# The 16-head attention stage of a two-layer decoder: ScalarE copies the projected keys out of PSUM instead of VectorE

## The chip, the cores and the metric

The kernel runs on one core of a Trainium2 chip. The metric is the device time of one execution in microseconds, lower is better. A core has TensorE (PE, matrix products), VectorE (DVE), ScalarE (ACT) and GpSimd (POOL), each with its own instruction queue in program order; SyncE (SP) here only issues DMA transfers. The engines wait for each other through semaphores. TensorE writes its results to PSUM, eight banks of 128 partitions by 512 float32 values, and VectorE and ScalarE read them there.

## The reference

Everything is float32. Tokens: batch 4, sequence 512, width 256. The decoder has two layers; after each block comes `x = layernorm(x + block(x))`.

```python
x = LN(x + L0_attn(x))            # one head of 256, rotary table
x = LN(x + L0_xattn(x, ctx))      # one head of 256, causal and padding mask
x = LN(x + L0_ffn(x))             # mixture of 8 experts, top 2
x = LN(x + L1_attn(x))            # 16 heads of 16, causal
x = LN(x + L1_xattn(x, ctx))      # 16 heads of 16, mask per query and key
x = LN(x + L1_ffn(x))             # 6 small layers: local attention and gated MLP
```

The two blocks of 16 heads, which the change touches, compute (the second with the context for keys and values and with biases on all projections):

```python
q, k, v = split(x @ Wq.T), split(x @ Wk.T), split(x @ Wv.T)   # (B, 16, 512, 16)
scores = einsum('bhqd,bhkd->bhqk', q, k) / sqrt(16)
scores = where(causal, -1e9, scores)      # cross: where(mask == 0, -1e9, scores)
out = einsum('bhqk,bhkd->bhqd', softmax(scores), v)
return merge(out) @ Wo.T                  # cross: + bo
```

## The kernel before, in words

The kernel is a row of stages. `stage_wide` does the two attentions of 256, `stage_moe` the experts, `stage_heads` both attentions of 16 heads, and `stage_l1_ffn` the six small layers, which take most of the time. The change lies in `stage_heads` alone, from about 486 to 1212 us.

`stage_heads` goes through eight batches of 512 tokens: four of the self attention (`j` 0 to 3), then four of the cross attention (`j` 4 to 7, `cross(j)` is true). A batch is 16 groups, `n` = 0 to 15: four query tiles `t` of 128 tokens, and in each four groups of four heads. In a self batch a tile `t` needs only `(t + 1) * 128` keys, in a cross batch all 512.

`body()` writes the order of the steps out by hand, once for a batch, and every engine walks through the same list, doing its own part of each step. The second entry of a step is the batch that it works for, relative to the one at hand: the projections of the next batch (offset 1) lie between the groups of this one. A prologue (`it` = -1) does them for the first batch, and the last batch has none to do. The steps of a group are, in this order:

- `s`: PE computes the scores of the four heads (L1988) into banks 4 to 7. It first waits until all four are drained.
- `max` 0 to 3: VectorE adds the mask and takes the row maximum (L2172), which drains a score bank; behind the fourth it scales the maxima for ScalarE (`h_nb`, L2177).
- `e` 0 to 3: ScalarE takes the exponentials of the group before (L2087), with a read of the row sum.
- `pt` 0 to 3: PE transposes the probabilities of the second-last group (L1998) into banks 2 and 3 in turn; ScalarE copies numbers 0 and 2 to `h_pT`, VectorE 1 and 3 (L2055).
- `pv`: PE multiplies probabilities and values of the third-last group (L2022).
- In between (`first` in the code, behind `max` 1, `e` 1 and `pt` 1): `q` and `k`, a projection on PE (L1964) into bank 0, then its copy to `h_qT` by ScalarE (L2074 with a bias, L2077 without) or to `h_kT` by VectorE (L2124 with, L2127 without); every fourth group (3, 7, 11, 15) `den` and `div`, where ScalarE copies the raw output (`h_o_raw`, L2102) and VectorE divides it (`h_oT`, L2201); one group later `wo`, the output projection.

The key steps `k` stand in groups 2, 6, 10 and 14, those of the queries in 1 and 9:

```python
            units = {1: ("q", 0), 2: ("k", 0), 6: ("k", 1), 9: ("q", 1), 10: ("k", 2), 14: ("k", 3)}
...
            yield from [("max", 0, n, 0), ("max", 0, n, 1), ("pt", of(m), m, 0), ("e", of(e), e, 0),
                        ("e", of(e), e, 1), ("pt", of(m), m, 1), *first, ("max", 0, n, 2), ("max", 0, n, 3),
                        ("pt", of(m), m, 2), ("e", of(e), e, 2), ("e", of(e), e, 3), ("pt", of(m), m, 3), *second]
```

In the self batches the input of the attention is itself still being made, from the sums of the experts' outputs: GpSimd fetches rows by an indirect DMA into `s_got`, VectorE adds them up (L1364) and normalises (L1382). These steps (`mix`) stand in groups 6 and 12 of the first two batches, and in the prologue.

Of the kernel before, what the change touches and what calls it, by code (L numbers as in the profile page):

```python
# [7 lines left out]
ALU = mybir.AluOpType  # L8
ACT = mybir.ActivationFunctionType
# [1728 lines left out]
def stage_heads(nc, shared, w_self, w_cross, preload, expert_sum):  # L1738
# [15 lines left out]
    with ExitStack() as ctx:  # L1754
# [9 lines left out]
        kT = sb("kT", [P, 2, QC, S])  # L1764
        v = sb("v", [P, 2, 2, TB, D])
# [74 lines left out]
        for step in full:  # L1840
            kind = step[0]
# [16 lines left out]
        def cross(j):  # L1858
            return j >= NB
# [6 lines left out]
        phases, ps = [], None  # L1866
        for it in range(-1, BODIES + 1):
            ps = Psum(shared, it, ps, True)
# [19 lines left out]
        def wait_filled(eng, ps, key, it):  # L1888
            eng.wait_ge(ps.sem_filled(key), ps.count(key, it))
# [168 lines left out]
        def _(act):  # L2058
            act.wait_ge(w_self["landed"], w_self["loads"])
            for steps, ps, it in phases:  # L2060
                if it == NB - 1:
                    act.wait_ge(w_cross["landed"], w_cross["loads"])
                for step in steps:
                    kind, off = step[:2]
                    j = it + off
# [4 lines left out]
                    elif kind == "q":  # L2070
                        e = step[2]
                        wait_filled(act, ps, step, it)
                        if cross(j):
                            ins = nc.scalar.activation(qT[:, j % 2, e, :], ps.ap(step), ACT.Identity,  # L2074
                                                       bias=w_cross["bq"][:, e:e + 1])
                        else:
                            ins = nc.scalar.copy(qT[:, j % 2, e, :], ps.ap(step))  # L2077
                        ins.then_inc(ps.sem_drained(step), 1)
                    elif kind == "e":
                        m, i = step[2:]  # L2080
                        n = group(it, m)
# [23 lines left out]
        def _(dve):  # L2105
# [3 lines left out]
            for b in range(2):  # L2109
                for parity in range(2):  # L2110
                    ins = nc.vector.memset(of_parity(v[:, b, parity], 1 - parity), 0.0)
            ins.then_inc(pads, 1)
            dve.wait_ge(w_self["landed"], w_self["loads"])
            for steps, ps, it in phases:
                if it == NB - 1:
                    dve.wait_ge(w_cross["landed"], w_cross["loads"])
                for step in steps:
                    kind, off = step[:2]
                    j = it + off
                    if kind == "k":  # L2120
                        e = step[2]
                        wait_filled(dve, ps, step, it)
                        if cross(j):
                            ins = nc.vector.tensor_scalar(kT[:, j % 2, e, :], ps.ap(step), w_cross["bk"][:, e:e + 1],  # L2124
                                                          None, ALU.add)
                        else:
                            ins = nc.vector.tensor_copy(kT[:, j % 2, e, :], ps.ap(step))  # L2127
                        ins.then_inc(ps.sem_drained(step), 1)
                    elif kind == "v":
                        i = step[2]  # L2130
                        wait_filled(dve, ps, step, it)
                        src = ps.ap(step).rearrange("p (t d) -> p t d", t=2)
                        for parity in range(2):
                            out = of_parity(v[:, j % 2, parity, 2 * i:2 * i + 2, :], parity)
                            if cross(j):
                                bias = w_cross["bv"][:].unsqueeze(1).broadcast_to([P, 2, D])
# [365 lines left out]
```

## Time and profile before

| | before |
|---|---|
| device time, median of 3 runs | 4149.62 us |
| the 3 runs | 4148.56 to 4154.87 us |
| the profiled execution, its own time | 4142.27 us |
| its span, first to last instruction | 4140.4 us |
| mean granted TensorE clock | 0.979 of full |
| busy PE / DVE / ACT / POOL | 3869.0 / 2905.0 / 2580.3 / 1239.8 us |

A row of the timeline gives the start in us from the span's beginning, the busy time, the engine, the line, the operation with the tile that it writes and those that it reads, shape and count (PE rows of one kind are merged, and a float32 matmul makes two of them). In brackets stands how long the engine was idle before it, and which instruction ended that. Busy shares are means over stages with different limits, so a stage is read from its own stretch.

### The profile page before, as it was taken

Reading aid. Unit: us, or ns where it says so; the run is one execution under the profiler, and the core shown is the slowest. Engines: PE = TensorE matmul, PEld = TensorE weight load, DVE = VectorE, ACT = ScalarE, POOL = GpSimd, SP = SyncE. Lnnn points to the kernel's source line nnn. Section 1 sums busy time; section 2 is a strip of 40 time slices with the busy share of each in tenths; the row PEclk is TensorE's granted clock in tenths of the full one; section 3 lists DMA queues with packets and bytes.
Section 4 is the critical chain, followed back from the end, with each engine's and each line's share of the span. In section 5 each row is a group of like instructions: output and inputs, shape, how many; then the busy total and the mean of one; then the engine's idle time right before and its main releaser. Section 6 shows DMA issues by size and latency. Waiting matters only on the chain.

```text
span 4140.4 us, 97849 instructions
## 1 busy us (share of the span) xinstructions
PE 3869.0 (93%) x36632; PEld 2539.5 (61%) x36632; DVE 2905.0 (70%) x10279; ACT 2580.3 (62%) x6856; POOL 1239.8 (30%) x809
## 2 busy tenths in 40 slices
PE   8979787899988999999999999999999999999996
PEld 5658554566655566666666666666666666666664
DVE  3542377788868878777777777777777777777773
ACT  2213265677756767667677676776766767767662
POOL 1103200000015443434343434343434343434330
PEclk9979899999999999999999999999999999999998
DMA  6002300000011001110011101110011101111010
GB/s 182 24 21 76 111 7 8 14 17 19 7 53 25 17 22 53 28 41 19 17 52 27 43 17 54 30 34 23 23 47 32 38 22 43 28 40 29 17 37 18
DMA packets 110784, 146.32 MB, mean 35 GB/s; under 512 B 35748, under 2 KB 77200, under 8 KB 109936
## 3 DMA queue, kind: packets, MB, share of 16 engines
q1 hardware_dynamic: 106912, 130.76, 11.1%
q0 software_dynamic: 3408, 9.31, 0.9%
q8 instruction: 299, 4.90, 0.5%
q14 instruction: 165, 1.35, 0.1%
HBM read 78.31 MB, written 11.40 MB: 22 GB/s over the span
## 4 chain that ended last, share of the span: by engine, by line
PE 54%; DVE 10%; POOL 4%; issue 2%; DMA 1%; ACT 0%; SPq 0%; DVEq 0%; POOLq 0%
PE psum L489 17%; PE psum L586 10%; PE psum L469 7%; PE psum L570 6%; PE psum L603 5%; PE psum L549 4%; PE psum L523 4%; POOL f_rn L892 3%; DVE f_rot L710 2%; DVE f_prob L753 1%; DVE f_rot L712 1%; DVE f_ss L717 1%; DVE f_xn L807 1%; PE psum L592 1%; DVE f_prob L781 1%
## 5 line engine op out<-in xcount | busy, mean ns | idle before, releaser
L489 PE MATMUL psum<-f_wqkv,f_xsT 128*128 128x512 f32 x2304 | 1073.0, 595 | 4.3 <-ACT f_raw L636 2.7
L887 POOL TENSOR_TENSOR f_raw<-f_rot 128x512 f32<-128x512 f32 x384 | 488.8, 1273 | 1662.4 <-DVE f_rot L712 1662.4
L650 ACT ACTIVATE f_prob<-f_prob,f_nb,f_rq 128x128 f32<-128x128 f32 x1536 | 740.0, 487 | 36.3 <-DVE f_nb L766 35.4
L489 PEld LDWEIGHTS psum<-f_wqkv,f_xsT 128*128 128x128 f32 x2304 | 402.5, 191 | 333.9 <-issue 329.0
L892 POOL TENSOR_TENSOR f_rn<-f_ss,f_half_pow 128x32 f32<-128x32 f32 x96 | 524.4, 5462 | 11.2
L586 PE MATMUL psum<-f_xnT,f_w 128*128 128x512 f32 x960 | 436.9, 594 | 2.2 <-ACT f_hT L673 1.1
L753 DVE CUSTOM_DVE_ANT_0 f_prob<-psum,f_band 128x128 f32<-128x128 f32 x1536 | 352.7, 285 | 114.9 <-PE psum L523 113.8
L634 ACT ACTIVATE f_sq<-psum 128x512 f32<-128x512 f32 x384 | 227.8, 593 | 230.2 <-PE psum L489 230.2
L781 DVE TENSOR_SCALAR f_prob<-f_prob,f_rs 128x128 f32<-128x128 f32 x1536 | 341.4, 286 | 13.5
L570 PE MATMUL psum<-f_wo,f_oT 128*128 128x256 f32 x1536 | 347.4, 379 | 1.6 <-ACT f_v L636 0.9
L710 DVE TENSOR_TENSOR f_rot<-f_raw,f_tab 128x512 f32<-128x512 f32 x384 | 333.0, 867 | 14.8 <-DMA x_before_mlp<-x_all 14.8
L570 PEld LDWEIGHTS psum<-f_wo,f_oT 128*128 128x128 f32 x1536 | 289.8, 190 | 71.3 <-issue 35.7
L2087 ACT ACTIVATE h_prob<-h_prob,h_nb 128x512 f32<-128x512 f32 (+3 forms) x512 | 324.7, 639 | 0.0
L586 PEld LDWEIGHTS psum<-f_xnT,f_w 128*128 128x128 f32 x960 | 178.9, 191 | 209.3 <-issue 200.3
L650 ACT ACTIVATION_READ_ACCUMULATOR f_prob<-f_prob,f_nb,f_rq 128x1 f32 x1536 | 294.7, 192 | 0.0
L1998 PE MATMUL psum<-ident,h_prob 128*128 128x128 f32 x1664 | 247.5, 280 | 50.2 <-DVE h_pT L2055 36.3
L1998 PEld LDWEIGHTS psum<-ident,h_prob 128*128 128x128 f32 x1664 | 182.0, 141 | 176.9 <-issue 94.1
L661 ACT COPY f_oT<-psum 128x512 f32<-128x512 f32 x192 | 111.5, 581 | 285.3 <-PE psum L549 285.2
L683 DVE COPY f_pT<-psum 128x512 f32<-128x512 f32 x192 | 131.9, 687 | 190.1 <-PE psum L469 189.8
L2055 ACT COPY h_pT<-psum 128x512 f32<-128x512 f32 (+3 forms) x256 | 129.0, 504 | 216.3 <-PE psum L1998 215.7
L712 DVE TENSOR_TENSOR f_rot<-f_raw,f_tab 128x512 f32<-128x512 f32 x384 | 262.4, 683 | 0.0
L717 DVE TENSOR_REDUCE f_ss<-f_sq 128x8 f32<-128x512 f32 x384 | 259.9, 677 | 0.0
(247 smaller groups left out, 7080.7 us busy)
## 6 DMA issues: line engine op xcount, KB each, us to landing
f_v_near<-f_v SPq DMA_DIRECT2D x168, 256.0 KB, 3.4
f_wqkv<-in_Wqkv SPq DMA_DIRECT2D x36, 512.0 KB, 6.7
w_moe_W<-in_L_ffn_W SPq DMA_DIRECT2D x2, 4096.0 KB, 23.5
f_w<-in_W SPq DMA_DIRECT2D x12, 640.0 KB
f_wo<-in_Wo SPq DMA_DIRECT2D x6, 1024.0 KB, 6.4
f_xs<-x_all SPq DMA_DIRECT2D x24, 254.0 KB
expert_rows<-m_y SPq DMA_DIRECT2D x39, 128.0 KB, 1.7
h_mask_int<-in_mask_BxSxS_ik SPq DMA_DIRECT2D x16, 256.0 KB
```

Source lines behind the costliest of these rows:

```text
L489: mm = nc.tensor.matmul(ps.ap(step), xsT[:, c, t * P:(t + 1) * P], wqkv[:, c, i * HALF:(i + 1) * HALF], start=c == 0, stop=c == KC - 1)
L570: mm = nc.tensor.matmul(ps.ap(step)[:, 0:D], oT[:, c, :], wo[:, c, :], start=c == 0, stop=c == OC - 1)
L586: mm = nc.tensor.matmul(ps.ap(step), w1[:, c, at:at + P], xnT[:, c, :], start=c == 0, stop=c == KC - 1)
L650: ex = nc.scalar.activation(pr, pr, ACT.Exp, bias=nb[:, t % 2, h:h + 1], scale=rq8[:, t, h:h + 1], accum_out=sums[:, t % 2, h:h + 1])
L710: nc.vector.tensor_tensor(heads(rot[:, n % 2, 0, :]), heads(q), cos, ALU.mult)
L712: nc.vector.tensor_tensor(rot[:, n % 2, 1, :].rearrange("p (h two d) -> p h two d", two=2, d=DH // 2), swapped, sin.rearrange("p h (two d) ...
L753: red = nc.vector.tensor_tensor_reduce(prob[:, (4 * n + 2 * j + i) % 16, :], ps.ap(key)[:, (n % 2 * 2 + j) * P:(n % 2 * 2 + j + 1) * P], b ...
L781: ins = nc.vector.tensor_scalar(pr, pr, rs[:, t % 2, h:h + 1], None, ALU.mult)
L887: nc.gpsimd.tensor_tensor(raw[:, (4 * t + i) % 8, :], rot[:, n % 2, 0, :], rot[:, n % 2, 1, :], ALU.add).then_inc(rope_done, 1)
L892: nc.gpsimd.tensor_tensor(rn[:, t % 2, :], ss[:, t % 2, :], half_pow[:], ALU.pow).then_inc(rn_ready, 1)
L1998: mm = nc.tensor.transpose(ps.ap(step)[:, k * P:(k + 1) * P], prob[:, n % 3 * HPC + i, k * P:(k + 1) * P], ident[:])
L2087: nc.scalar.activation(pr, pr, ACT.Exp, bias=nb[:, t % 2, h:h + 1], scale=scale, accum_out=sums[:, t % 2, h:h + 1]).then_inc(exp_ready, 1)
```

## The change

For the step `k` the branch moves from VectorE's program to ScalarE's. Without a bias ScalarE makes a copy, with one an activation of the kind Identity with the bias column. What is waited for and what is signalled is the same. TensorE's, GpSimd's and SyncE's programs are unchanged.

```diff
@@ scalar @@
                             ins = nc.scalar.copy(qT[:, j % 2, e, :], ps.ap(step))
                         ins.then_inc(ps.sem_drained(step), 1)
+                    elif kind == "k":
+                        e = step[2]
+                        wait_filled(act, ps, step, it)
+                        if cross(j):
+                            ins = nc.scalar.activation(kT[:, j % 2, e, :], ps.ap(step), ACT.Identity,
+                                                       bias=w_cross["bk"][:, e:e + 1])
+                        else:
+                            ins = nc.scalar.copy(kT[:, j % 2, e, :], ps.ap(step))
+                        ins.then_inc(ps.sem_drained(step), 1)
                     elif kind == "e":
@@ vector @@
-                    if kind == "k":
-                        e = step[2]
-                        wait_filled(dve, ps, step, it)
-                        if cross(j):
-                            ins = nc.vector.tensor_scalar(kT[:, j % 2, e, :], ps.ap(step), w_cross["bk"][:, e:e + 1],
-                                                          None, ALU.add)
-                        else:
-                            ins = nc.vector.tensor_copy(kT[:, j % 2, e, :], ps.ap(step))
-                        ins.then_inc(ps.sem_drained(step), 1)
-                    elif kind == "v":
+                    if kind == "v":
                         i = step[2]
```

VectorE's order at the key step of group 2 of the second cross batch, as a piece of the difference. The rows L2055 and L2172 around it are the copy of transposed probabilities 1 and the masked maximum 2 with its read-out.

```order
 L2172 ISA h_mx 128x1
 L2055 COPY h_pT<-psum 128x512
-L2124 TENSOR_SCALAR h_kT<-psum,w_x_bk 128x512
 L2172 ISA h_prob,h_mx<-psum,h_add_mask 128x512
 L2172 ISA h_mx 128x1
```

The key copy is gone from between them; the rest of VectorE's order is the same.

ScalarE's order at the same place after the change, where the exponentials stand on L2096 and the key copy with its bias on L2083.

```order
L2055 COPY h_pT<-psum 128x512
L2096 ACTIVATE h_prob,h_sums<-h_prob,h_nb 128x512 x2
L2083 ACTIVATE h_kT<-psum,w_x_bk 128x512
L2055 COPY h_pT<-psum 128x512
L2096 ACTIVATE h_prob,h_sums<-h_prob,h_nb 128x512 x2
```

The row L2083 is new; without it the two exponentials were followed at once by the copy of transposed probabilities 2.

ScalarE's order in the prologue, before (first piece) and after (second piece).

```order
L2069 COPY h_xT<-psum 128x512 x2
L2077 COPY h_qT<-psum 128x512 x2
L2069 COPY h_xT<-psum 128x512 x2
```

```order
L2069 COPY h_xT<-psum 128x512 x2
L2077 COPY h_qT<-psum 128x512
L2086 COPY h_kT<-psum 128x512 x2
L2077 COPY h_qT<-psum 128x512
L2086 COPY h_kT<-psum 128x512 x2
L2069 COPY h_xT<-psum 128x512 x2
```

Four key copies have come in here, two behind each query copy.

## Rows read from the trace of the kernel before

**Rows 1.** Groups by form, VectorE, then ScalarE (busy, mean ns | idle before, releaser).
```profile
L2124 DVE TENSOR_SCALAR h_kT<-psum,w_x_bk 128x512 f32<-128x512 f32 x16 | 12.0, 748 | 9.6 <-PE psum L1964 9.6
...
L2127 DVE COPY h_kT<-psum 128x512 f32<-128x512 f32 x16 | 11.0, 689 | 17.2 <-PE psum L1964 17.2
...
L2074 ACT ACTIVATE h_qT<-psum,w_x_bq 128x512 f32<-128x512 f32 x8 | 5.5, 688 | 2.1 <-PE psum L1964 2.1
L2077 ACT COPY h_qT<-psum 128x512 f32<-128x512 f32 x8 | 4.7, 587 | 17.5 <-PE psum L1964 13.7 <-remote 3.8
```
**Rows 2.** One stretch: length, busy us PE, PEld, DVE, ACT, POOL, PE clock, DMA.
```profile
937.00:1031.00 94.00, 86.86 (x988) 58.44 (x978) 76.35 (x218) 66.33 (x169) 3.49 (x2) 1.00 0.06 18
```
**Rows 3.** Who waited for whom, 500 to 770 us, then 770 to 1190.
```profile
PE psum L1988 <- DVE h_mx L2172: 12.7, 22, 1.1
...
PE psum L1988 <- DVE h_mx L2172: 16.4, 34, 0.7
```
**Rows 4.** Timeline, second cross batch: end of group 1, group 2, start of group 3.
```profile
936.21 1.07 PE L2022 MATMUL psum<-h_pT,h_v 128*32 128x128 f32 x31
...
937.21 1.14 PE L1988 MATMUL psum<-h_kT,h_qT 32*128 32x512 f32 x8
...
939.21 1.88 PE L1964 MATMUL psum<-h_srcT,w_x_Wk 128*128 128x512 f32 x4
...
941.13 0.75 DVE L2124 TENSOR_SCALAR h_kT<-psum,w_x_bk 128x512 f32<-128x512 f32 x1 [0.74 <-PE psum L1964]
941.57 0.59 ACT L2055 COPY h_pT<-psum 128x512 f32<-128x512 f32 x1 [0.59 <-PE psum L1998]
...
941.90 1.08 PE L2022 MATMUL psum<-h_pT,h_v 128*32 128x128 f32 x32
...
943.13 0.17 DVE L2177 TENSOR_SCALAR h_nb<-h_mx 128x4 f32<-128x4 f32 x1
...
943.25 1.14 PE L1988 MATMUL psum<-h_kT,h_qT 32*128 32x512 f32 x8 [0.27 <-DVE h_mx L2172]
...
945.01 0.59 ACT L2055 COPY h_pT<-psum 128x512 f32<-128x512 f32 x1 [1.44 <-PE psum L1998]
```
**Rows 5.** Timeline, starts of groups 2 and 3 of the last batch.
```profile
1122.72 1.14 PE L1988 MATMUL psum<-h_kT,h_qT 32*128 32x512 f32 x8
...
1127.61 1.14 PE L1988 MATMUL psum<-h_kT,h_qT 32*128 32x512 f32 x8
```
**Rows 6.** Timeline, what follows groups 6, 10, 14 (third self batch), 6 (cross).
```profile
709.85 0.71 PE L1988 MATMUL psum<-h_kT,h_qT 32*128 32x256 f32 x8 [0.52 <-DVE h_mx L2172]
...
710.97 0.37 ACT L2055 COPY h_pT<-psum 128x256 f32<-128x256 f32 x1 [1.16 <-PE psum L1998]
...
727.32 0.93 PE L1988 MATMUL psum<-h_kT,h_qT 32*128 32x384 f32 x8 [0.60 <-DVE h_mx L2172]
...
748.87 1.14 PE L1988 MATMUL psum<-h_kT,h_qT 32*128 32x512 f32 x8 [0.43 <-DVE h_mx L2172]
...
967.07 1.14 PE L1988 MATMUL psum<-h_kT,h_qT 32*128 32x512 f32 x8 [0.24 <-DVE h_mx L2172]
```
**Rows 7.** Timeline, after group 6 of the first, second and fourth self batch.
```profile
536.00 0.71 PE L1988 MATMUL psum<-h_kT,h_qT 32*128 32x256 f32 x8 [0.77 <-DVE h_mx L2172]
...
619.50 0.48 DVE L1364 SCALAR_TENSOR_TENSOR x_all<-s_got,s_gates,x_all 128x256 f32<-128x256 f32 x1 [1.25 <-DMA s_got<-expert_rows,s_slot_int]
...
785.34 0.71 PE L1988 MATMUL psum<-h_kT,h_qT 32*128 32x256 f32 x8 [0.58 <-DVE h_mx L2172]
```
**Rows 8.** Timeline, prologue's end and first groups.
```profile
508.27 1.40 DVE L1382 TENSOR_SCALAR x_all<-x_all,s_mv,s_rstd 128x256 f32<-128x256 f32 x4 [1.16 <-POOL s_rstd L1354]
...
509.59 0.67 DVE L2127 COPY h_kT<-psum 128x512 f32<-128x512 f32 x1
...
510.47 0.81 PE L1988 MATMUL psum<-h_kT,h_qT 32*128 32x128 f32 x8 [4.37 <-DVE h_kT L2127]
...
518.35 0.59 ACT L2077 COPY h_qT<-psum 128x512 f32<-128x512 f32 x1 [3.78 <-remote]
```
## The prediction

> **What bounds the kernel now.** I read the page first, then the stage of the change through the busy times of a stretch, the list of waits, and the timeline of single groups. Over the stretch of [rows 2], which lies in the 512-key part, TensorE (PE) is busy for 86.86 of 94 us, VectorE (DVE) for 76.35 and ScalarE (ACT) for 66.33. No engine is full. PE is nearest to it, and ACT has the most room: 28 us in 94. What PE loses, it loses where a group hands over to the next: the score matmuls (L1988) wait for VectorE's last row maximum of the group before, because all four score banks must be drained. In the list of waits this is 12.7 us in 22 waits up to 770 us and 16.4 us in 34 waits after it [rows 3], 29.1 us together. That sum is the most that a lighter VectorE can give back there, and a part of it belongs to groups in which no keys are copied.
>
> The timeline of one group with a key copy shows the order of events [rows 4]. The scores start at 937.21. PE projects the keys from 939.21 to 941.09 and VectorE, idle for 0.74 us until then, copies them from 941.13. Only behind that copy come its maxima 2 and 3. The scaled maximum (L2177) starts at 943.13, and the next scores start at 943.25, after PE has waited 0.27 us. PE's last work of the group, the probabilities times the values (L2022), started at 941.90 and took 1.08, so it was over at 942.98. So VectorE is the later one here, and it is late by the key copy: it stood idle until the projection was there, though the scores for its maxima had long been filled.
>
> **What the change removes.** VectorE loses 16 plain copies of 689 ns and 16 with a bias of 748 ns, 23.0 us of busy time [rows 1]. Its maxima 2 and 3 no longer queue behind the projection. In the group of [rows 4] they may start 1.4 us earlier (the idle 0.74 and some 0.66 until the next start), more than PE's wait. PE's own work then sets the start of the next scores, and the gain is the wait that stands on that row. It was there because of VectorE alone: the last batch has no key projection, and there group 2 lasts from 1122.72 to 1127.61, 4.89 us [rows 5], against 6.04 us in [rows 4] (937.21 to 943.25). The difference, 1.15 us, is less than the projection's 1.88 us, since part of the projection fills gaps of PE.
>
> There are 32 key copies: 4 in the prologue and 4 in each of the seven batches that prepare a next one. By place:
> - Cross batches 1 to 3 (512 keys): 0.27 us at groups 2, 10 and 14 [rows 4], which repeat, and 0.24 us at group 6 [rows 6]. 1.05 us a batch, 3.2 us in all.
> - Third self batch: 0.52, 0.60 and 0.43 us at groups 6, 10 and 14 [rows 6]. At group 2 PE did not wait, so I count nothing. 1.6 us. The fourth is the same with 0.58 at group 6 [rows 7], 1.6 us.
> - Second self batch: 0.60 and 0.43 as before, 1.0 us. Group 6 gives nothing, because VectorE stands in group 7 for expert rows that GpSimd fetches: 1.25 us before the first of eight additions [rows 7], and the others wait too. An earlier VectorE only waits longer.
> - First self batch: 0.77 us at group 6 [rows 7], 0.60 and 0.43 behind it, and for group 2, which stands beside a stall (below), 0.6 by its neighbour, group 10. 2.4 us.
> - Prologue: the first scores (510.47) waited 4.37 us for the fourth key copy [rows 8], which VectorE could do only behind a normalisation that began at 508.27 and took 1.40. ScalarE is free there, so the scores move ahead of the end of the normalisation. Then VectorE's maxima can start at 509.67 and the transposes queued on PE behind the scores can too, against 510.47 plus the scores' own 0.81 before, that is up to 1.6 us. I take 1.5.
>
> The sum is 3.2 + 1.6 + 1.6 + 1.0 + 2.4 + 1.5 = 11.3 us. Where PE does not wait its rows overlap by 0.07 us (the row at 936.21 ends at 937.28, the scores start at 937.21 [rows 4]), and 24 hand-overs may gain that on top, 1.7 us at most. Between 11.3 and 13.0 I take 12.5 us.
>
> **What it adds.** ScalarE gets 32 instructions. Its nearest rows are the query copies, the same forms from the same PSUM banks: 587 ns plain and 688 ns with a bias [rows 1], so 16 × 0.587 + 16 × 0.688 = 20.4 us of busy time. In its order the key copy stands ahead of the copy of transposed probabilities 2, with exponentials 2 and 3 and, in the next group, the copy of transposed probabilities 0 behind it. In the group of [rows 4] that probability copy started at 941.57 after 0.59 us of idle time, since PE issues its transposes behind the key projection. The keys are full at 941.09, so the new copy begins in this hole at about 941.13 and pushes the probability copy to at most 941.82, by 0.25 us. The exponentials behind it end as much later. Nobody meets them before group 3, in which ScalarE stood idle for 1.44 us until PE's transposes came (945.01, [rows 4]). With PE's start 0.27 earlier and ScalarE 0.25 later, 0.9 us are left. The tightest of the other places is group 7 of the self batches: 1.16 us of idle time [rows 6], less 0.52 for the earlier start and at most 0.3 for the later end. The cost on the path is nothing as long as these holes stand. If the cover were gone, each copy would cost its 0.59 to 0.69 us. The next group after each key group is a divide group (3, 7, 11, 15) and its length hangs on ScalarE's chain, which starts with PE's scores. So that group keeps its length, and what the key group gained stays gained.
>
> No wait is added to PE or to a DMA queue. The bank of the keys is drained by whichever engine copies them, at about the same moment.
>
> **The rivals.**
> *It gains less, within 0.2%.* The first groups stand beside stalls that no engine of this kernel releases: ScalarE waited 3.78 us at 518.35 "remote" [rows 8]. If that stall ends at a fixed moment, the prologue's 1.5 us and the first group 2's 0.6 are lost, and if the 0.07 do not add, 11.3 − 2.1 = 9.2 us are left. One more half-clock stretch of PE, or half of the gains in the self batches (6.6 us by the list) missing, brings it to some 6 us: 4143.6 us.
> *It gains more.* Were VectorE the bound in key groups and just behind them, each copy would give back all its time: 23.0 us less the 2.8 of the prologue, 20 us, 4129.6 us. For it speaks that the waits of [rows 3] sum to 29.1 us. Against it, PE in [rows 4] is late by itself 0.27 us earlier.
> *It gets slower.* ScalarE's copies land on the chain of the divide groups: copy 0, two exponentials, the raw output copy, then VectorE's division and maxima. This decides once ScalarE comes later than PE's transposes, that is when its delay exceeds the idle time left in [rows 4] and [rows 6]. Then 28 copies cost 16 × 0.688 + 12 × 0.587 = 18.1 us and nothing is gained: 4167.7 us. The 0.59 us hole and the 1.16 and 1.44 us behind it speak against this.
> The Trainium skill says in "ScalarE: Activation LUTs", Rules for kernel authors, that an addition is work for VectorE and not for ScalarE; by that rule the change would lengthen the work that it moves. In [rows 1] the same forms take 688 ns against 748 and 587 against 689, so here the measurement decides against the rule.
> The Trainium skill's "Runtime: NRT & Kernel Launch", Instruction fetch mechanics, has each engine fetch its instructions in blocks of 256, mostly hidden; 32 more on ScalarE and 32 fewer on VectorE would move the places of such fetches, and no row shown ties the "remote" stall to them.
>
> **How the numbers follow.** The gain of about 12.5 us: 0.62. More, some 20 us: 0.08. Less, some 6 us: 0.22. Slower: 0.08. The profiled execution took 4142.27 us, and the sum makes that 4129.8. It lies 7.35 us under the median of the runs shown, 4149.62, from which I subtract the same 12.5: 4137. The range reaches from the rival with more (4129.6, less a little for the half-clock stretches, whose places move with the time) to a gain close to nothing: 4128 to 4149. The slower rival is left out. 0.2% of this time, 8.3 us, is about what a measurement of this kernel can tell from no change. Faster by more than that: 0.70, within it 0.22, slower 0.08.
>
> **What the profile would show.** VectorE has 32 instructions and 23 us less in the stage. The wait of the scores for VectorE after groups 2, 10 and 14 of a cross batch is gone and such a group lasts 5.7 instead of 6.04 us, while the divide groups keep theirs. The key copy on ScalarE starts within 0.1 us of the projection's end, and ScalarE's idle time before copy 0 of the next group is shorter but not gone. The prediction is wrong if that idle time is zero, if a new wait of PE for ScalarE's probability copy appears, or if the stall near 518 us grows.

## The result, and the profile after

| | before | changed |
|---|---|---|
| median of 20 runs each, taken together | 4152.34 us | 4143.08 us |
| lowest and highest | 4141.97 to 4158.32 | 4139.10 to 4152.14 |
| profiled execution, its own time / its span | 4142.27 / 4140.4 us | 4144.43 / 4142.4 us |
| mean granted TensorE clock of that execution | 0.979 | 0.974 |

The ratio is 0.9983, with the interval 0.9976 to 0.9989: the change is faster, by 0.17%, some 7 us (the means, 4151.7 and 4144.1, lie 7.6 us apart, the medians 9.3). Two later comparisons, which stand with the experiments, gave 0.9979 [0.9970, 0.9988] and 0.9977 [0.9968, 0.9986], that is 9 to 10 us. The profiled execution of before is as fast as the fastest of its 20 runs (4141.97) and had a higher clock, 0.979, than any of the 105 later runs of that kernel (0.973 to 0.978). So its span cannot be compared with the one of after. What can be compared are groups of the stage in which both ran at full clock.

The page of the changed kernel gives the load of each engine:

```profile
span 4142.4 us, 97849 instructions
...
PE 3881.6 (94%) x36632; PEld 2548.2 (62%) x36632; DVE 2886.2 (70%) x10247; ACT 2602.4 (63%) x6888; POOL 1240.4 (30%) x809
```

VectorE lost 19 us of 2905, ScalarE gained 22 of 2580. The groups by form show the new instructions (busy, mean ns | idle before, releaser), against [rows 1]:

```profile
L2083 ACT ACTIVATE h_kT<-psum,w_x_bk 128x512 f32<-128x512 f32 x16 | 11.0, 689 | 3.7 <-PE psum L1964 2.5
...
L2086 ACT COPY h_kT<-psum 128x512 f32<-128x512 f32 x16 | 9.4, 588 | 15.5 <-PE psum L1964 15.3
```

Here they take 689 and 588 ns, 20.4 us in all, where 688 and 587 were expected from the query copies. The stretch of [rows 2], read again:

```profile
937.00:1031.00 94.00, 87.89 (x1001) 58.77 (x989) 74.13 (x215) 69.76 (x176) 3.48 (x2) 1.00 0.06 18
```

In 94 us PE works 1.03 us more, VectorE 2.2 less, ScalarE 3.4 more. The list of waits, up to 770 us and then from 770 to 1190, answers to [rows 3]:

```profile
PE psum L1988 <- DVE h_mx L2172: 6.8, 12, 0.7
...
PE psum L1988 <- ACT h_kT L2086: 0.9, 1, 0.9
...
PE psum L1988 <- DVE h_mx L2172: 12.6, 19, 0.7
```

The waits of the scores for VectorE's maxima fell from 29.1 us in 56 waits to 19.4 us in 31. None of the 31 that are left stands at the start of group 3, 7, 11 or 15, that is behind a key group. The timeline of the second cross batch shows the same group as [rows 4]:

```profile
937.31 1.14 PE L1988 MATMUL psum<-h_kT,h_qT 32*128 32x512 f32 x8
...
939.31 1.88 PE L1964 MATMUL psum<-h_srcT,w_x_Wk 128*128 128x512 f32 x4
...
941.01 0.68 DVE L2172 CUSTOM_DVE_ANT_0 h_prob<-psum,h_add_mask 128x512 f32<-128x512 f32 x1
...
941.23 0.69 ACT L2083 ACTIVATE h_kT<-psum,w_x_bk 128x512 f32<-128x512 f32 x1
...
941.74 0.17 DVE L2177 TENSOR_SCALAR h_nb<-h_mx 128x4 f32<-128x4 f32 x1
941.82 0.58 ACT L2055 COPY h_pT<-psum 128x512 f32<-128x512 f32 x1
...
942.00 1.08 PE L2022 MATMUL psum<-h_pT,h_v 128*32 128x128 f32 x32
...
943.01 1.14 PE L1988 MATMUL psum<-h_kT,h_qT 32*128 32x512 f32 x8
...
944.77 0.59 ACT L2055 COPY h_pT<-psum 128x512 f32<-128x512 f32 x1 [0.96 <-PE psum L1998]
```

VectorE's fourth maximum starts at 941.01, before the projection has even ended (941.19). The scaled maximum is there 4.43 us after the scores, against 5.92 before. The next scores start at 943.01 with no wait, right behind the products with the values: 5.70 us instead of 6.04. ScalarE copies the keys in the hole that it had, passes 0.15 us of delay to its probability copy (4.51 us after the scores, 4.36 in [rows 4]), and is idle for 0.96 us before copy 0 of the next group, where it was 1.44.

The lengths of the groups, from one start of the scores to the next, before and after; where there are several batches of a kind they agree to 0.02 us:

| | group 2 | 6 | 7 | 10 | 14 | whole batch |
|---|---|---|---|---|---|---|
| third self | 3.88, 3.75 | 4.67, 4.09 | 4.08, 4.09 | 5.28, 4.61 | 5.98, 5.48 | 74.97, 73.10 |
| fourth self | 3.94, 3.75 | 5.02, 4.37 | 4.51, 5.17 | 5.34, 4.61 | 6.03, 5.48 | 76.04, 74.58 |
| first cross | 6.03, 5.70 | 6.40, 6.09 | equal | 6.03, 5.70 | 6.04, 5.70 | 94.27, 92.61 |
| second cross | 6.03, 5.70 | 6.40, 6.09 | equal | 6.04, 5.70 | 6.04, 5.70 | 93.91, 92.60 |

(In the first cross batch group 12 went from 6.98 to 6.62 too; see the end.)

### The profile page after: what moved, and what is told of

It reads as the page before. It is cut to its first block, busy times and chain, and to the rows that moved or that the text cites. A ratio compares the mean times of both kernels' runs of the same rounds, so it can differ in the third digit from the quotient of the medians.

```text
span 4142.4 us, 97849 instructions
## 1 busy us (share of the span) xinstructions
PE 3881.6 (94%) x36632; PEld 2548.2 (62%) x36632; DVE 2886.2 (70%) x10247; ACT 2602.4 (63%) x6888; POOL 1240.4 (30%) x809
## 4 chain that ended last, share of the span: by engine, by line
PE 55%; DVE 9%; POOL 4%; issue 2%; DMA 1%; ACT 0%; SPq 0%; DVEq 0%; POOLq 0%
PE psum L489 18%; PE psum L586 10%; PE psum L469 7%; PE psum L570 6%; PE psum L603 5%; PE psum L549 4%; PE psum L523 4%; POOL f_rn L892 3%; DVE f_rot L710 2%; DVE f_prob L753 1%; DVE f_rot L712 1%; DVE f_ss L717 1%; DVE f_xn L807 1%; PE psum L592 1%; DVE f_prob L781 1%
## 5 line engine op out<-in xcount | busy, mean ns | idle before, releaser
L892 POOL TENSOR_TENSOR f_rn<-f_ss,f_half_pow 128x32 f32<-128x32 f32 x96 | 524.1, 5459 | 11.2
L2096 ACT ACTIVATE h_prob<-h_prob,h_nb 128x512 f32<-128x512 f32 (+3 forms) x512 | 325.7, 641 | 0.0
L469 PE MATMUL psum<-ident,f_prob 128*128 128x128 f32 x1536 | 244.1, 282 | 10.7 <-DVE f_prob L781 9.8
```

Source lines behind the costliest of these rows:

```text
L469: mm = nc.tensor.transpose(ps.ap(key)[:, slot * P:(slot + 1) * P], src, ident[:])
L892: nc.gpsimd.tensor_tensor(rn[:, t % 2, :], ss[:, t % 2, :], half_pow[:], ALU.pow).then_inc(rn_ready, 1)
L2096: nc.scalar.activation(pr, pr, ACT.Exp, bias=nb[:, t % 2, h:h + 1], scale=scale, accum_out=sums[:, t % 2, h:h + 1]).then_inc(exp_ready, 1)
```

## The experiments

There are three series, each on a chip of its own. In each the kernel before ran on that chip too, and the ratios are to it: medians of 4153.44 us (26 runs), 4153.74 (33) and 4153.18 (35). "Batch 0" below is the time from the stage's first transposes (`psum<-ident,x_all`) to the first scores of the second self batch, so it takes in the prologue's end.

### First series: controls, and two theories on what was lost

**The kernel before, unchanged.**

> The kernel before, unchanged, as a control: its ratio to itself shows what this measurement can tell, expected 1.000 within 0.002. Theory A (the stretches of TensorE at its lower clock level vary from execution to execution) expects another total of such stretches than the 180 us of the first trace, and group lengths in the cross batches equal to 0.02 us. Theory B (the longer 217 us after the change are the change's doing) expects 180 us again.

Measured: 4153.65 us, ratio 1.0001 [0.9992, 1.0010], span 4151.6, clock 0.975. TensorE stood at the lower of its two clock levels for 206 us in this profile, and for 180 in the one that the prediction was made from, so this varies from one execution to the next, as theory A has it. Batch 0 lasts 103.62 us here and 101.05 in the first profile; the two later kernels that leave the key copies in this batch's groups on VectorE have 103.29 and 103.82, so the first profile was the odd one. The batches from the second on agree with the first profile to 0.2 us, those from the third on to 0.02.

**The changed kernel, unchanged.**

> The changed kernel, unchanged, as a control. Expected ratio 0.9975 to 0.999. Theory A expects another total of low-clock stretches than 217 us, and with it other lengths in the first two self batches, while the third self batch and the cross batches keep theirs (the gains of 0.67, 0.59, 0.50 and 0.34 us). Theory B expects 217 us and the loss in groups 0 to 4 of the first self batch again.

Measured: 4143.52 us, 0.9979 [0.9970, 0.9988], span 4143.5. Against the control's span that is 8.1 us. TensorE's time at the lower level is 217 us again, as theory B has it (and 220 in a third profile, below), some 10 us more than in the control. Each theory is right in a part: the first profile of before was low by chance, and the changed kernel has more of that time than the control. The third self batch and the cross batches keep their gains.

**The bias addition of GpSimd in group 2 instead of group 6.** In the fourth self batch the gain of group 6 is lost in group 7 (table above). The timeline of the changed kernel there:

```profile
785.61 1.11 POOL L2243 TENSOR_TENSOR h_rstd<-h_rstd,half_pow 128x4 f32<-128x4 f32 x1 [72.21 <-DVE h_rstd L2219]
...
786.69 2.37 POOL L2248 TENSOR_TENSOR x_all<-x_all,w_x_bo 128x1024 f32<-128x1024 f32 x1
...
787.59 1.49 DVE L2177 TENSOR_SCALAR h_nb<-h_mx 128x4 f32<-128x4 f32 x1
...
787.72 0.71 PE L1988 MATMUL psum<-h_kT,h_qT 32*128 32x256 f32 x8
...
789.00 0.41 DVE L2055 COPY h_pT<-psum 128x256 f32<-128x256 f32 x1
```

The scaled maximum, 128 by 4 values, takes 1.49 us instead of 0.17, and ends at 789.08, when GpSimd's addition (786.69 + 2.37 = 789.06) ends. The copy queued behind it is as late. The kernel before meets the same addition there, but later in it:

```profile
783.67 2.36 POOL L2248 TENSOR_TENSOR x_all<-x_all,w_x_bo 128x1024 f32<-128x1024 f32 x1
...
785.23 0.82 DVE L2177 TENSOR_SCALAR h_nb<-h_mx 128x4 f32<-128x4 f32 x1
```

Its scaled maximum takes 0.82 us and ends at 786.05, the addition at 786.03. So the stall was there before the change, and the change, by which VectorE arrives earlier, made it longer.

```diff
                 if n == 6:
-                    yield from [("norm", -1), ("bo", 1)]
+                    yield ("norm", -1)
+                if n == 2:
+                    yield ("bo", 1)
```

> The changed kernel with GpSimd's addition of the output bias placed at group 2 instead of group 6. If VectorE's scaled maximum of group 6 in the fourth self batch ends late because GpSimd's 2.4 us addition holds it (theory lock), that row falls from 1.49 us to 0.17 and groups 6 and 7 of that batch get 0.66 us shorter together; another VectorE instruction may be held in its place near group 0. If VectorE is late for its own work (rival), the two groups keep their length. The total changes by less than 1 us either way, below what the timing tells.

Measured: 4139.73 us (9 runs), 0.9968 [0.9958, 0.9978]. The timeline at the same place:

```profile
782.17 0.17 DVE L2179 TENSOR_SCALAR h_nb<-h_mx 128x4 f32<-128x4 f32 x1
...
782.29 0.71 PE L1990 MATMUL psum<-h_kT,h_qT 32*128 32x256 f32 x8
...
786.38 0.93 PE L1990 MATMUL psum<-h_kT,h_qT 32*128 32x384 f32 x8 [0.27 <-DVE h_mx L2174]
```

The scaled maximum takes 0.17 us again and group 7 lasts 4.09 us instead of 5.17. The batch falls from 74.58 to 73.49. So 1.1 us were lost to GpSimd in the changed kernel, shown: 0.66 us by the change, and the rest was lost in the kernel before already (4.51 us, where group 7 of the third self batch has 4.08). The expectation had the cause right and the size, 0.66, too small. As it allowed, other scaled maxima are held in this one's place: one in each of the first three cross batches takes 1.63 to 1.65 us (at 830.81, 923.42 and 1016.03), and there it costs nothing, the batches last 92.60 and 92.61 us.

The rest of this kernel's better time is not explained by its edit: its profile, which is of the fastest of its 9 runs, has batch 0 at 96.51 us against 99.80 and 100.28, and in that batch the two programs are the same, since the addition occurs only where a cross batch comes next.

**VectorE keeps the copy, behind its maxima.** This is the kernel before with one reordering of VectorE's list; nothing moves to ScalarE.

```diff
+        def key_copies_late(steps):
+            out, held = [], []
+            for step in steps:
+                if step[0] == "k" and any(s[0] == "max" for s in steps):
+                    held.append(step)
+                    continue
+                out.append(step)
+                if step[0] == "max" and step[3] == HPC - 1:
+                    out += held
+                    held = []
+            return out + held
...
-                for step in steps:
+                for step in key_copies_late(steps):
```

> The kernel before, with the key copy still on VectorE but behind the fourth maximum of its group instead of ahead of the third. Theory order (the gain is that the maxima no longer queue behind the projection): the cross groups 2, 10 and 14 take 5.70 us as after the change, and most of the gain of the 28 copies in the groups is there, 6 to 9 us, the prologue's 1.5 us not. Theory load (the gain is VectorE's smaller load): they stay near 6.04 us, or the following group gets longer by what this one gained, and the total stays at that of before.

Measured: 4140.09 us (6 runs), 0.9967 [0.9955, 0.9979], more than the 6 to 9 us expected (see the repeat in the third series). The timeline of its second cross batch:

```profile
931.87 1.14 PE L1988 MATMUL psum<-h_kT,h_qT 32*128 32x512 f32 x8
...
936.30 0.17 DVE L2189 TENSOR_SCALAR h_nb<-h_mx 128x4 f32<-128x4 f32 x1
936.38 0.75 DVE L2136 TENSOR_SCALAR h_kT<-psum,w_x_bk 128x512 f32<-128x512 f32 x1
...
936.55 1.08 PE L2022 MATMUL psum<-h_pT,h_v 128*32 128x128 f32 x32
937.04 0.68 DVE L2055 COPY h_pT<-psum 128x512 f32<-128x512 f32 x1
937.57 1.14 PE L1988 MATMUL psum<-h_kT,h_qT 32*128 32x512 f32 x8
```

5.70 us as well, with VectorE as loaded as before, and the whole cross batch lasts 92.60 us as in the changed kernel. What the change removes there is a place in a queue, not work. The late copy has a small price of its own: group 7 is longer than in the changed kernel by 0.35 us in the third self batch and by 0.64 in the fourth, which lasts 75.22 us against 74.58.

### Second series: ScalarE's cost, the prologue, and the parts

**ScalarE reads each key bank twice.** A second copy into a spare tile ahead of each of the 28 key copies outside the prologue:

```diff
                     elif kind == "k":
                         e = step[2]
                         wait_filled(act, ps, step, it)
+                        if it >= 0:
+                            nc.scalar.copy(spare[:], ps.ap(step))
```

> The changed kernel, in which ScalarE reads each key bank of the 28 key steps in the groups twice: first a plain copy into a spare tile that nobody reads, then the key copy. That adds 28 copies of 587 ns, 16.4 us of ScalarE's time. Theory hole (ScalarE has idle time before the first copy of the next group, 0.4 us or more is left of it after the change) expects the group lengths to stay within 0.1 us in the cross batches and at most 0.3 us more in groups 3, 7 and 11 of the self batches: under 4 us in all. The rival (ScalarE is at its limit in the key groups) expects each extra copy on the path, 0.48 to 0.59 us each, 13 to 16 us in all.

Measured: 4142.83 us, 0.9977 [0.9968, 0.9986]. Its group by form, and then its timeline:

```profile
L2084 ACT COPY h_spare<-psum 128x512 f32<-128x512 f32 x28 | 16.4, 587 | 8.9 <-PE psum L1965 6.7
```

```profile
937.95 1.14 PE L1989 MATMUL psum<-h_kT,h_qT 32*128 32x512 f32 x8
...
941.87 0.59 ACT L2084 COPY h_spare<-psum 128x512 f32<-128x512 f32 x1
...
942.35 0.69 ACT L2086 ACTIVATE h_kT<-psum,w_x_bk 128x512 f32<-128x512 f32 x1
...
942.93 0.59 ACT L2056 COPY h_pT<-psum 128x512 f32<-128x512 f32 x1
...
943.64 1.14 PE L1989 MATMUL psum<-h_kT,h_qT 32*128 32x512 f32 x8
...
945.41 0.59 ACT L2056 COPY h_pT<-psum 128x512 f32<-128x512 f32 x1 [0.48 <-PE psum L1999]
```

16.4 us more on ScalarE cost next to nothing: the group has its 5.69 to 5.70 us, the cross batches keep their 92.6 us, and the third and fourth self batch are longer by only 0.07 and 0.13 us. The idle time before the next copy 0 halves to 0.48 without reaching zero. The rival in which the copies land on ScalarE's chain is out, with as much again in hand.

**The prologue's four copies back on VectorE.** `elif kind == "k" and it >= 0` on ScalarE, and VectorE's old branch for `it < 0`.

> The changed kernel with the four key copies of the prologue back on VectorE. Theory: the first scores wait for the fourth key copy again and group 1 starts 26.3 us after the stage's first transposes as before the change, not 25.0; all groups from the second self batch on keep the lengths of the changed kernel. The timing shows 0 to 1.5 us more than the changed kernel. The rival (the prologue's early start pushes the first groups into a stretch of TensorE at its lower clock and costs what it gains) expects group 5 to start as early or earlier than in the changed kernel, 38 to 43 us after the first transposes.

Measured: 4142.58 us, 0.9977 [0.9968, 0.9987], the same as the changed kernel. Its group 1 starts 26.37 us after the stage's first transposes, 24.96 in the changed kernel, but the second self batch starts at 100.18 against 100.28. One thing was not as expected: group 3 of the fourth self batch lasts 3.53 us instead of 3.18, in this profile and in a later one of the same kernel. VectorE's division there starts after 1.20 us of waiting for ScalarE's raw output copy, 0.84 in the changed kernel. The cause was not followed; a shift of the same size is told at the end.

**Both better ideas together**, the late VectorE copy with the early bias addition:

> The key copies on VectorE behind the fourth maximum, and GpSimd's bias addition at group 2: a candidate. Expected: the group lengths of the run with late key copies, but group 7 of the fourth self batch back from 5.81 to 4.5 us, so 1.0 to 1.3 us less than that run; ratio to before 0.995 to 0.998. Theory load would see no gain at all over the kernel before.

Measured: 4141.80 us, 0.9976 [0.9967, 0.9984]. The fourth batch lasts 73.92 us, 1.3 less than with the late copy alone, so the two gains do add there. The time is not below either of the two, which speaks against reading their 4140 us as real.

**Only the 16 copies with a bias moved** (`kind == "k" and cross(j)`): the fourth self batch and the first three cross batches.

> The change for the keys of the four cross batches alone (16 copies with a bias, in the fourth self batch and the first three cross batches); the 16 of the self batches stay on VectorE. Theory: the terms add, so the fourth self batch lasts 1.5 us less and the first three cross batches 1.3 us less each, 5.4 us in all, and the batches before keep the lengths of the kernel before: ratio 0.9987. The rival (the gain comes from elsewhere, from the first batches) expects 1.000.

Measured: 4148.33 us, 0.9990 [0.9980, 0.9999]. The cross batches last as in the changed kernel. The fourth self batch has the shorter groups 2, 6, 10 and 14, but loses it in groups 7 and 8 (5.74 and 4.67 instead of 4.51 and 3.94): 75.89 us against 76.04 before, where 1.5 less was expected. A scaled maximum is held here too, for 1.48 us. So the terms of the cross batches add as expected, and that of the fourth self batch depends on when VectorE meets GpSimd's addition.

### Third series: does the clock take something back?

In the first series the changed kernel's runs showed a mean clock lower by 0.0010 than those of before. In the second series the kernel with the doubled copy had 0.0014 less, and the one with the prologue on VectorE only 0.0002 less. The standard error of such a difference, from the scatter of the runs, is 0.0002 to 0.0004. This series asks whether the lower clock is real, and whether the prologue is its cause.

**Only the prologue's four copies on ScalarE**, the other 28 as before (the cut shows ScalarE's line against the changed kernel; VectorE keeps its old branch for `it >= 0`):

```diff
-                    elif kind == "k":
+                    elif kind == "k" and it < 0:
```

> Only the prologue's four key copies are on ScalarE, the other 28 stay on VectorE. Theory that the mean granted clock pays the prologue's move back: group 1 starts 24.9 to 25.0 us after the stage's first transposes instead of 26.2 to 26.4, the runs' mean clock lies below that of the kernel before by 0.0005 to 0.001, and the median is within 2 us of the kernel before, on either side. Rival, that the prologue's 1.3 us persist and nothing is paid: same clock as before and a median 1 to 2 us below. A third, that the move costs time outright: over 3 us slower.

Measured: 4151.80 us, 0.9997 [0.9989, 1.0006]; mean clock of its runs 0.97567, of before in the same series 0.97617. The stretch of batch 0 in the kernel before (the control), in this one, in the changed kernel, and in the one with the prologue alone on VectorE (columns as in [rows 2]; the first figure behind the stretch is its length, the clock stands third from the end):

```profile
492.13:595.75 103.62, 84.66 (x596) 50.05 (x597) 66.50 (x245) 47.86 (x159) 17.59 (x18) 0.85 0.24 79
```

```profile
492.67:596.49 103.82, 84.86 (x596) 49.69 (x597) 64.36 (x241) 50.21 (x163) 17.64 (x18) 0.85 0.24 79
```

```profile
492.63:592.91 100.28, 84.21 (x596) 49.16 (x597) 61.83 (x237) 52.02 (x167) 17.65 (x18) 0.86 0.25 82
```

```profile
496.52:596.70 100.18, 81.70 (x597) 48.28 (x597) 64.31 (x241) 49.79 (x163) 17.66 (x18) 0.87 0.25 82
```

The prologue's move alone changes batch 0 by 0.2 us, in the wrong direction. Its first scores come 3.5 us sooner (20.02 instead of 23.52 after the first transposes), group 1 1.4 us sooner (24.72 and 26.16), and by group 5 nothing is left (42.82 and 42.36). Against the control 0.76 us go in group 1 (4.04 and 3.28) and 1.46 in group 2 (5.48 and 4.02). In that group VectorE stands idle, and the profile names no engine of this kernel as what ended it, but "remote":

```profile
524.21 0.29 DVE L2055 COPY h_pT<-psum 128x128 f32<-128x128 f32 x1 [1.75 <-remote]
```

The median is 1.4 us below that of before, within an interval that reaches from 4.6 less to 2.5 more, so the timing can't tell the predicted 1.5 us from nothing.

**The other kernels again.** First the changed one with the prologue on VectorE, then the changed one, then the late copy.

> The changed kernel with the prologue's four key copies back on VectorE, once more and now beside the changed kernel on one chip. Theory that the prologue's move lowers the clock: mean clock as the kernel before (within 0.0004), and 0.0005 to 0.001 above the changed kernel's; median 0 to 3 us below the changed kernel's. Rival, that the clock of the changed kernel is lower because of all its copies, or by chance: the two show the same clock.

Measured: 4143.44 us, 0.9976 [0.9967, 0.9984], mean clock 0.97525. That is 0.0009 below before, where the theory of the prologue wanted at most 0.0004, and 0.0006 above the changed kernel's.

> The changed kernel once more, beside the kernel before and the three others. At equal clock it should be 11 to 14 us below the kernel before, as in the two earlier comparisons, and over all runs 8 to 11 us, since its mean clock was lower by 0.0006 to 0.001 there. If the lower clock was chance, the two show the same clock here and the medians lie 11 to 14 us apart.

Measured: 4143.54 us, 0.9977 [0.9968, 0.9986], mean clock 0.97464.

> The kernel before with VectorE's key copies queued behind the fourth maximum, now with more runs and beside the changed kernel. If it is really better than the changed kernel, its median lies 2 to 4 us below it again and its mean clock is that of the kernel before, since its prologue is that of before. If the first result was chance, the two agree within 1 us.

Measured: 4143.17 us (11 runs), 0.9980 [0.9971, 0.9988], mean clock 0.97482. It equals the changed kernel; the lead that it had in its first 6 runs did not come again. That profile had batch 0 at 96.70 us, this one at 99.91.

The changed kernel's lower clock is real: 0.0010 and 0.0015 in the two series that have it, nearly four and nearly five standard errors. Sorted by the mean clock that each run shows, the means of all runs of the kernel before (three series) and of the changed one (these and its first 20), with the number of runs (the 26 runs of before at 0.977 and 0.978 have no partner):

| clock | before | changed | difference |
|---|---|---|---|
| 0.973 | 4162.1 us (4) | 4146.9 us (5) | 15.2 |
| 0.974 | 4159.2 us (8) | 4145.4 us (17) | 13.8 |
| 0.975 | 4154.6 (34) | 4142.8 (15) | 11.8 |
| 0.976 | 4152.9 (33) | 4140.7 (5) | 12.2 |
| all | 4153.75 (105), clock 0.97567 | 4144.09 (42), clock 0.97448 | 9.7 |

At an equal clock the two differ by some 12 to 15 us. A run of before loses 2.5 us per 0.001 of clock (a straight line through its 105 runs), so the 0.0012 that the changed kernel lacks answers to 3.0 us, and 9.7 + 3.0 = 12.7. This is a comparison of runs sorted by the clock that they had; no run held the clock fixed, so what it takes back is an estimate.

The profiles show where it could lie. From the stage's first transposes to its last scores there are 706.4 us in the control and 695.2, 695.2 and 694.7 in the three profiles of the changed kernel, 11.2 to 11.7 less. What follows, where the two programs are the same, takes 2953.1 us in the control and 2954.6, 2954.7 and 2954.2 in the changed one, 1.1 to 1.6 more. But it also takes 2950.1 in the first profile of before, and 2949.4 to 2954.1 in the nine profiles of the other kernels, so these few profiles do not prove it.

Why the clock is lower is open. The prologue's move alone lacks 0.0005, and the changed kernel 0.0006 against the one without that move, each about one and a half standard errors. The kernel without that move lacks 0.0002 in the second series and 0.0009 in the third; the late copy has 0.0002 more than before in the first (6 runs) and 0.0013 less in the third. So neither the prologue nor the shorter groups are shown as its cause.

## Why the prediction was right, and where its sizes were off

The forecast was 4137.0 us, the range 4128 to 4149; the changed kernel takes 4143.1. It is faster, but by 7 to 10 us and not by 12.5 against the kernel before of the same series. That is at the border which the prediction drew itself: it gave 0.70 to more than 0.2%, and the three comparisons have 0.17, 0.21 and 0.23%. The base was 4149.62, the median of three runs, while 20 runs give 4152.34 and the control 4153.65. Had the base been that, the same 12.5 would have made 4140 to 4141, which leaves a miss of 2 to 3 us. That the time falls almost on the figure of the rival "less", 4143.6, is owed to the same low base, and not to a gain of only 6 us.

- **Mechanism.** As written: VectorE late by its place in the queue, PE's own work next. The group of [rows 4] was to last 5.7 us and lasts 5.70. The reordering on VectorE alone gives the same group, which shows that it is the order.
- **Cross batches.** The term of 3.2 plus the overlap (0.07 at each of 12 hand-overs, 0.8) makes 4.0. Measured: 0.33, 0.31, 0.33 and 0.34 in the four key groups of a batch, 1.31 us, 3.9 in three, and 0.35 more at one group 12.
- **Third self batch.** 1.6 plus overlap; measured 1.87 in the table. Group 2, counted at nothing, gave 0.13.
- **Fourth self batch.** 1.6; measured 1.46. The gain at group 6, 0.65, was given back in group 7 as 0.66. VectorE, earlier now, meets GpSimd's addition nearer to its start and is held 0.67 us longer (1.49 against 0.82). So the step "what the key group gained stays gained" failed in this batch. I had looked for late engines only on PE, VectorE and ScalarE. The early bias addition gives it back.
- **Second self batch.** 1.0; measured 0.0 (91.99 and 92.19 before, 91.96, 92.45 and 91.88 after). Group 6 was absorbed in group 7 as predicted (4.67 to 4.09, then 14.97 to 15.55). Groups 10 and 14 are shorter by 0.67 and 0.1, and groups 8 and 13 longer by about as much (4.82 and 5.08 to 5.31 and more; 8.76 and 8.61 to 9.12). But group 13 has 9.11 also in the kernel that moved only the cross batches' copies, which leaves this batch as before. Why was not tested.
- **First self batch and prologue.** 2.4 + 1.5 = 3.9 taken; measured 103.62 in the control to 100.28, 99.80 and 99.89, 3.3 to 3.8 (against the first profile of before, 101.05, only 0.8 to 1.3). But it is divided otherwise: the prologue alone gives 0.2 us the wrong way, and without the prologue's move the other copies give all of it (100.18 and, in the second profile, 99.82). So no profile shows the prologue's term, and it went as the rival "less" had it. Two things stand against it. First, PE, having done its scores early, waits 2.26 us for the same normalisation as before (L1382), and the query projection behind it takes 3.44 us, at the lower of TensorE's two levels, where it took 2.65 before and 2.56 in the control:

```profile
515.69 1.97 PE L1952 MATMUL psum<-ident,x_all 128*128 128x128 f32 x8 [2.26 <-DVE x_all L1382]
...
518.38 3.44 PE L1964 MATMUL psum<-h_xT,w_a_Wq 128*128 128x512 f32 x4
...
531.61 3.58 PE L1976 MATMUL psum<-w_a_Wv,h_xT 128*128 128x256 f32 x8
```

  (The value projection at 3.58 us is no loss to the control, which has 3.51; only the first profile had 1.89.) Second, the "remote" idle time of [rows 8] comes back. Waits so marked, of 1.1 to 5.4 us on VectorE, ScalarE or both, stand at this place in ten of the fourteen profiles, among them the late copy's second one:

```profile
524.00 0.59 ACT L2077 COPY h_qT<-psum 128x512 f32<-128x512 f32 x1 [3.85 <-remote]
```

  In eight of the ten the first such wait ends 31.5 to 31.8 us after the stage's first transposes, with the prologue on either engine (31.59 in the first profile, 31.54 in the one shown and with the prologue moved alone, 31.74 in the changed kernel), as a stall that ends at a fixed moment would. In the control and in the changed kernel's second profile it is absent. So the rival's condition is borne out as far as these profiles go. What ends that wait they do not show.
- **ScalarE's cost.** Nothing, as taken. Doubling it costs 0.2 us in two self batches. The signs that would have spoken against the prediction did not appear: ScalarE's idle time before copy 0 is 0.96 us and not zero, and the stall near 518 us did not grow (3.78 us before; 1.59, none and 2.52 in the changed kernel).
- **Sum.** By rows of the stage: 3.5 + 0.0 + 1.9 + 1.5 + 4.3 = 11.2 us, against 11.3 before the overlap and 12.5 taken; 0.35 us of it is group 12, which no term had. The step that was mis-sized is the one from 11.3 to 12.5: the 0.07 us of overlap are there in the cross batches, but the second self batch (1.0), the prologue (1.5, in the sum with the first batch) and group 7 of the fourth gave less than their terms. What the timing shows less than 11.2, 1.5 us or so, goes with the lower clock; that a change of the program changes the clock was not in the sum, and why it did is open.

The rival "less" named one more stretch at the lower clock, and TensorE's time at the lower level is some 10 us longer than in the control; in that sense a part of it came true. "More" and "slower" did not. The rule of the Trainium skill on additions ("ScalarE: Activation LUTs", Rules for kernel authors) did not hold here: 689 ns on ScalarE against 748 on VectorE, float32 out of PSUM.

No variant beat the changed kernel for certain. The early bias addition has the best figure, 4139.73 us in 9 runs, and an interval that overlaps the changed kernel's. It was not run again, and the late copy's like figure did not hold when it was. Of its advantage 1.1 us is shown in a place.

## What to carry to other kernels

When an engine is late, ask what it waited in front of: here VectorE stood idle before a copy whose input came late, with ready work queued behind. Here moving that copy to another engine or behind that work gave the same, 0.1 to 0.7 us a group, so the load of the engine was not the point. The gain was lost again where the early engine met something with its own time (a gather in group 7 of the second self batch, a GpSimd addition in the fourth, a normalisation in the prologue), so follow the engine that is now early to its next wait. And where gains of 0.2% are at stake, one profile is not a base: take the change from segments that ran at full clock, and compare runs at the same mean clock as well as over all.

## What was not expected of the hardware

- GpSimd's addition of 128x1024 (2.37 us) held a VectorE instruction of 128x4 values, from 0.17 to 1.49 us; both end within 0.03 us of each other. The Trainium skill has a cause in "SBUF — State Buffer", SBUF: two separate sides: the two engines share a pair of ports, and a GpSimd instruction or a VectorE one in a two-port mode holds it for its whole length, whichever starts first. The trace agrees in that GpSimd started first and both end together; it does not show the mode of the VectorE instruction. The kernel before has 0.82 us at this place, meeting the addition later, and the kernel with the addition elsewhere has 0.17 here and 1.63 to 1.65 where the addition now stands.
- Group 12 of the first cross batch lasted 6.98 us with a first maximum that began late. In the kernel before:

```profile
901.26 1.14 PE L1988 MATMUL psum<-h_kT,h_qT 32*128 32x512 f32 x8 [0.74 <-DVE h_mx L2172]
902.88 0.69 DVE L2172 CUSTOM_DVE_ANT_0 h_prob<-psum,h_add_mask 128x512 f32<-128x512 f32 x1 [0.97 <-PE psum L1988]
```

With only the prologue's copies moved:

```profile
910.11 1.14 PE L1988 MATMUL psum<-h_kT,h_qT 32*128 32x512 f32 x8 [0.74 <-DVE h_mx L2181]
911.38 0.69 DVE L2181 CUSTOM_DVE_ANT_0 h_prob<-psum,h_add_mask 128x512 f32<-128x512 f32 x1 [0.62 <-PE psum L1988]
```

The maximum comes 1.62 us after the scores in the one and 1.27 in the other. All five profiles of kernels in which VectorE keeps its 32 copies have 6.98 us, late copy or not; all nine in which it has fewer have 6.62 or 6.63. So these 0.35 us go with the number of instructions that VectorE has done by then, four fewer being enough, and not with which copies are moved; that this number is the cause is argued and not tested. The Trainium skill's "Runtime: NRT & Kernel Launch", Instruction fetch mechanics, has each engine fetch its instructions in blocks of 256 and calls the cost mostly hidden. Such a fetch is a guess for these 0.35 us; the trace does not show one there.
- The mean granted clock of one and the same kernel varied from 0.973 to 0.978, and its time with it, from 4162.1 to 4148.9 us in the means. Profiles of batch 0 in kernels of like order fall in two lengths, some 100 us in eight and 96.5 to 96.7 in two, with the clock at 0.86 to 0.89. Neither of the two short ones has the "remote" idle time, but a profile of the changed kernel without it (99.80 us) has the long one. What decides it was not found.
